# ScalarE copies the next batch's keys behind the exponentials in the first layer

## What is computed

```python
a = _layer_norm(audio_kv, ln_gamma, ln_beta)          # 8 x 1500 x 256
Q = (hidden_states @ Wq.T).reshape(B, Tt, HEADS, HEAD_DIM).transpose(0, 2, 1, 3)
K = (a @ Wk.T).reshape(B, Ta, HEADS, HEAD_DIM).transpose(0, 2, 1, 3)
V = (a @ Wv.T).reshape(B, Ta, HEADS, HEAD_DIM).transpose(0, 2, 1, 3)
scores = jnp.einsum('bhtd,bhsd->bhts', Q, K) * scale
attn = jax.nn.softmax(scores, axis=-1)
out = jnp.einsum('bhts,bhsd->bhtd', attn, V)
return hidden_states + jnp.tanh(gate) * out
```

## Time and profile before

| | |
|---|---|
| Median of 3 runs | 1822.67 us (1819.48 to 1823.98) |
| The profiled execution, timed as the runs are | 1822.74 us |
| Its span, first to last instruction | 1820.9 us |
| PE busy | 1671.2 us (92%), mean granted clock 0.973 |
| DVE busy | 1214.3 us (67%) |
| ACT busy | 1041.7 us (57%) |
| POOL busy | 898.0 us (49%) |
| Mean DMA rate over the span | 82 GB/s |

### The profile page before, as it was taken

How to read it: one execution, slowest core, us unless ns; L and a number is a source line. 1 busy time by engine, 2 the same in 40 slices (tenths; PEclk the granted TensorE clock), 3 DMA queues, 4 the chain that set the end, 5 groups by cost and what they waited for, 6 DMA issues and landing times.

```text
span 1820.9 us, 40621 instructions
## 1 busy us (share of the span) xinstructions
PE 1671.2 (92%) x12520; PEld 1571.5 (86%) x12520; DVE 1214.3 (67%) x2334; ACT 1041.7 (57%) x2023; POOL 898.0 (49%) x655
## 2 busy tenths in 40 slices
PE   3698889887798999999999999989999999999997
PEld 2577777776688999999999997789999999999986
DVE  5477777766546667667766767466676676677673
ACT  2476666656454566565655656545565665656563
POOL 4455555533234365355445547544554653554483
PEclk8899999999889999999999999999999999999998
DMA  7766676775322111001101104221111010010021
GB/s 228 210 146 166 157 178 175 175 171 118 90 64 81 43 34 67 34 34 67 35 33 67 49 23 140 64 78 35 57 58 43 34 67 34 34 67 0 1 88 42
DMA packets 109911, 149.69 MB, mean 82 GB/s; under 512 B 25540, under 2 KB 95684, under 8 KB 109828
## 3 DMA queue, kind: packets, MB, share of 16 engines
q1 hardware_dynamic: 108484, 142.45, 28.0%
q10 hardware_dynamic: 1344, 6.19, 1.0%
HBM read 108.32 MB, written 3.42 MB: 61 GB/s over the span
## 4 chain that ended last, share of the span: by engine, by line
PE 63%; DVE 9%; SPq 6%; issue 4%; ACT 3%; DMA 2%; POOL 2%; DVEq 0%; ACTq 0%; POOLq 0%
PE ps L765 11%; PE ps L767 11%; PE ps L766 11%; PE ps L1016 7%; PE ps L1020 7%; PE ps L1018 7%; SPq L389 4%; PE ps L951 2%; DMA q<-q_scratch 2%; DVE ar L1851 1%; PE ps L996 1%; PE ps L983 1%; SPq L392 1%; DVE negm L1879 1%; ACT prob L1292 1%
## 5 line engine op out<-in xcount | busy, mean ns | idle before, releaser
L717 POOL TENSOR_TENSOR rr<-ar,rr 125x512 fp32r<-125x512 f32 x336 | 450.8, 1376 | 417.1 <-ACT rr L1474 401.1
L1016 PE MATMUL ps<-cx,rr 125*128 125x258 f32 x1344 | 395.5, 294 | 0.0
L1020 PE MATMUL ps<-cx,rr 125*128 125x258 f32 x1344 | 379.3, 282 | 0.0
L1018 PE MATMUL ps<-cx,rr 125*128 125x256 f32 x1344 | 379.2, 282 | 0.0
L765 PE MATMUL ps<-rr,ct 128*125 128x256 f32 x1152 | 330.6, 287 | 4.5 <-DVE ar L1896 2.7
L767 PE MATMUL ps<-rr,ct 128*125 128x256 f32 x1152 | 325.2, 282 | 0.0
L766 PE MATMUL ps<-rr,ct 128*125 128x256 f32 x1152 | 324.9, 282 | 0.0
L1018 PEld LDWEIGHTS ps<-cx,rr 125*128 125x128 f32 x1344 | 254.7, 190 | 0.0
L1020 PEld LDWEIGHTS ps<-cx,rr 125*128 125x128 f32 x1344 | 254.7, 190 | 0.0
L1016 PEld LDWEIGHTS ps<-cx,rr 125*128 125x128 f32 x1344 | 253.6, 189 | 0.1
L1461 ACT ACTIVATE ar<-ar 125x512 f32<-125x512 f32 x336 | 208.6, 626 | 78.2 <-DVE ar L1896 54.5
(11 more groups left out here) (210 smaller groups left out, 3743.2 us busy)
## 6 DMA issues: line engine op xcount, KB each, us to landing
raw_t<-in_ctx_t SPq DMA_DIRECT2D x24, 1500.0 KB, 6.3
k<-khl SPq DMA_DIRECT2D x192, 187.5 KB
raw<-in_ctx SPq DMA_DIRECT2D x16, 1500.0 KB
raw<-in_ctx SPq DMA_DIRECT2D x8, 1408.0 KB
raw<-stat_scratch ACTq DMA_DIRECT2D x7, 750.0 KB, 3.9
w_raw<-in_wq SPq DMA_DIRECT2D x32, 128.0 KB, 2.3
w_raw<-in_wk SPq DMA_DIRECT2D x32, 128.0 KB, 2.2
qo<-in_wqt SPq DMA_DIRECT2D x32, 128.0 KB, 2.4
```

Source lines behind the costliest of these rows:

```text
L717: pool.tensor_tensor(group(p[:, 1, :, :], u, k), x, f(group(p[:, 0, :, :], u, k)), ALU.subtract)\
L1016: pe.matmul(ps[:, bank, 0:D + 2], hi, cx[0:KC, c, 0:D + 2], start=c == 0, stop=False, skip_group_check=True)
L1018: pe.matmul(ps[:, bank, 0:D], hi, cx[0:KC, c, D + 2:CW], start=False, stop=False, skip_group_check=True)
L1020: mm = pe.matmul(ps[:, bank, 0:D + 2], lo, cx[0:KC, c, 0:D + 2], start=False, stop=c == CH - 1, skip_group_check=True)
```

## The change

In ACT's `slot` the copy of the keys moves from ahead of the exponential to behind the exponential and `output`. It issues the same instructions with the same waits. It applies in slots 0 to 5 of batches 0 to 6, 42 copies. The other engines' programs are unchanged.

```diff
--- before.py
+++ after.py
@@ -1335,10 +1335,6 @@
                     if u_last == 0 and later:
                         act.wait_ge(s["zpv"], SLOTS * b)
                     values(b + 1 if t else b, u_last, 1 - n if t else n, 6)
-                if t in K_AT and kind != "plain":
-                    u = K_N[t]
-                    act.wait_ge(s["zkl"], 6 * (b + 1) + u - 4)
-                    keys(b + 1, u, 5)
                 if kind == "full" and t == 4:
                     spread_stats(b + 2)
                 if not (kind == "plain" and t == SLOTS - 1):
@@ -1347,6 +1343,10 @@
                     softmax(n if t < SLOTS - 1 else 1 - n, (t + 1) % SLOTS, g + 1)
                 if t or later:
                     output(g - 1)
+                if t in K_AT and kind != "plain":
+                    u = K_N[t]
+                    act.wait_ge(s["zkl"], 6 * (b + 1) + u - 4)
+                    keys(b + 1, u, 5)
                 high_probs(g, 0)
                 high_probs(g, 1)
                 if kind == "full":
```

## The result

| | before | changed |
|---|---|---|
| Median | 1823.98 us (1818.86 to 1831.35, 7 runs) | 1834.23 us (1827.15 to 1845.85, 7 runs) |
| Ratio to before | | 1.0066 [1.0039, 1.0093] |
| Profiled execution | 1822.74 us | 1827.37 us |
| Its span and mean granted clock | 1820.9 us, 0.973 | 1825.5 us, 0.970 |

The sign of the likeliest case was right, its size was not: +4.85 us forecast, about +10 to +12 us measured by medians and ratio. The profiled execution of the changed kernel is +4.63 us on the profiled one of before, but it is the second fastest of its seven, so that agreement is worth little. The seven changed runs also line up with their clocks: 1827.15 us at 0.969, 1845.85 us at 0.957.

A forecast was written before the change was run, and what follows sets the result against it. It took a 50.3 us loop through SP's stacks, POOL and L775 to bound the first layer. +6.65 at batch 6's landing, −2.1 and +0.3 gave +4.85 us on 1822.74 (median 1822.67), forecast 1827.6, range 1821 to 1832.

The forecast's parts named there:

- the likeliest case: Whole kernel: the sum of terms as it stands, +4.85 us to 1827.6 us, spanning 1825 to 1830.5; chance 45%.
- The loop, its owner and the step of 1.70 us: First layer: SP's stacks, POOL, L775 and the keys' copy form a 50.3 us loop; slot 4's later copy adds 1.70.
- The exponential: ACT: starts 0.6 us earlier in slot 4, 0.35 us in other slots, saving 0.35 at L775 in batches 0 to 2.
- rival B: L775: longer waits drop PE's clock, each fall costing about 2 us; one gives 1829.7, two 1831.8; chance 25%.
- the sum: First layer: +6.65 us at the landing in batch 6, −2.1 given back, +0.3 for pair 0, making +4.85 us.
- the slack of batches 0 to 2: L775 of batches 1 and 2 still waits for DVE, so full 1.70 us steps add only from batch 4 on.
- the give-back in batch 6: Batch 6: PE no longer waits for the exponential behind the copy, returning 1.6 to 2.6 us, taken as 2.1.
- The wait for pair 0: Batch 7's first scores: SP's stack of pair 0 comes 1.7 us later, costing 0 to 1.7 us, taken as 0.3.
- C: Stacks: transfers bound them, not SP's issuing; earlier statistics broadcast shortens the burst by 1.2 us; 1821.9 us; chance 13%.
- D: Stacks: the stretch to the last landing gives up 1.7 us, landings don't move, only gains remain; 1819.8 us; chance 10%.
- The range: Whole kernel: 1821 to 1832 us, leaving out D and the far end of rival B.

The follow-up runs named there:

- e1: Changed kernel with the keys' copy back ahead of the exponential in slot 4 only; 1824.94 us, 1.0010 of the kernel before.
- e2: Kernel before with the keys' copy behind the exponential in slot 4 alone; 1837.51 us, 1.0078 of the kernel before.
- e8: Kernel before with one extra, unused subtraction on POOL ahead of slot 4's key block; 1827.01 us, 1.0023 of the kernel before.
- e6: Changed kernel with eight unused matmuls on PE ahead of L775 in batches 0 to 5; 1832.59 us, 1.0045 of the kernel before.
- e13: Changed kernel with eight unused matmuls on PE ahead of L775 in batches 1 to 5 only; 1833.56 us, 1.0048 of the kernel before.
- e15: Second measurement of the changed kernel with eight unused matmuls ahead of L775 in batches 0 to 5; 1833.45 us, 1.0043 of the kernel before.
- e3: The changed kernel measured and profiled once more, nothing else altered; 1839.85 us, 1.0071 of the kernel before.
- e5: Kernel before with POOL's variance of slot 2 computed ahead of its third key block and `ra`; 1819.58 us, 0.9975 of the kernel before.
- e11: Kernel before with POOL's variance early and six unused matmuls in PE's waits of slot 6; 1818.93 us, 0.9965 of the kernel before.
- e12: Second measurement of the kernel before with POOL's variance ahead of its third key block and `ra`; 1818.51 us, 0.9967 of the kernel before.
- e4: Changed kernel with POOL's variance of slot 2 computed ahead of its third key block and `ra`; 1822.78 us, 1.0000 of the kernel before.
- e14: Changed kernel with eight unused matmuls ahead of L775 in batches 1 to 5 and six in slot 6; 1838.62 us, 1.0064 of the kernel before.

## Why the prediction was wrong

**The loop, its owner and the step of 1.70 us: right.** Landing to SP's start went from 14.53 to 16.27 us, POOL's wait in slot 4 from 3.19 to 4.88 us (forecast 4.9), and e1 and e2 put the loss on slot 4. e8 made a third of it without ACT. Starts 52.0 us apart were forecast from batch 2 on and are there on average where the clock holds behind L775 (52.0 to 52.1 us in e6, e13, e15).

**The exponential: its shift right, and worth nothing.** It came 0.6 us earlier in slot 4. L775 waited 0.57 us for DVE in batch 1 in place of 0.88, as forecast, but that wait had no weight once POOL was the last. e1, which keeps the earlier exponential in the other slots, gains nothing (1.0010).

**Step that failed, the largest: the clock behind L775 (rival B at 25%, with one or two falls, and left out of the sum).** I let a single row decide, the wait of 3.00 us at 401.38 that left the clock at full, and gave B a quarter. The runs show a fall behind the loop's longer waits at L775 as a rule: two in the first profile of the changed kernel, five in e3, four in e2. The price of one, "about 2 us", was right: 1.3 to 2.3 us from landing to SP's start. Their number was not. Holding the clock there gives back some 3 to 5 us. The Trainium skill, TensorE: Matmul & The Clock Gate, Part 1: The HAM clock gate, has the clock go back to 1.2 GHz when the array idles; I quoted it as making B near certain, and here the rows of 2.90, 3.57, 3.79 and 4.19 us agree with it. No wait of that length at L775 did as the row at 401.38 had done.

**Step that failed, second: the slack of batches 0 to 2.** I let the loop take hold in batch 3, since batch 0 showed 34.36 us from SP's start to the landing and batch 1 34.67. Over the 17 profiles of this case the stretch of batch 0 is 34.03 to 37.11 us and 35.61 on average, that of batch 1 34.67 to 37.16 and 36.02: one of my two was among the shortest, the other the shortest of all. With the average of batch 0, L775 of batch 1 waits for POOL already, which takes 1.15 us out of the slack; with that of batch 1, L775 of batch 2 does too, another 0.95 us. The last landing then moves by 8.75 us, not 6.65 (an estimate, from the averages and the prediction's own rules). So it is in e3 (152.82, 2.99 us for POOL) and in e15, where batch 0 to batch 1 takes 52.24 us, in place of the 50.7 (50.14 + 0.55) that I had worked out. In e6, e15 and e13 the last landing lies 7.5, 7.8 and 7.9 us behind before's profile.

**Step that failed, third: the give-back in batch 6, taken as 2.1 us.** The exponential no longer makes PE wait, as forecast, but the end doesn't come earlier. From the last landing to the layer's end it is 74.2 us in the first profile of the changed kernel in place of 75.3. That one profile misleads: over the eleven profiles that have the copy behind the exponential in slots 3 and 5 it is 74.1 to 77.1 us and 75.6 on average, over the five with the old order (before, e5, e8, e11, e12) 74.8 to 75.8 and 75.4. I had forecast 1.8 us less. All eleven have a wait for the low part of the probabilities in its place, 1.68 to 4.86 us at L847 (3.00 in e3, 3.34 in e15), and none of the five has one. The wait for pair 0 stands in four of the eleven (0.30 to 1.71 us), which fits the 0.3 on average.

**The sum again.** 4.85, plus 2.1 for the slack and 1.8 for a give-back that isn't there, is 8.75 us. The kernels with the clock held at L775 stand at +7.8 to +8.8 us by their ratios, and end the layer 6.2, 6.7 and 9.3 us behind before's profile (490.6, 491.0, 493.7). The falls at L775 add 3 to 5, and 12 to 14 is where the changed kernel measured +12 and +13 us by its two ratios. So nothing large is left over, but each of these terms is known to 1 us at best.

**C and D** are out: no stretch of stacks gave up anything (34.03, 37.07, 35.53, 34.53 and 36.04 us against 34.36, 34.67, 36.58, 35.78 and 36.01), and the broadcast of the statistics issued earlier didn't shorten it. Single stretches of 32.9 to 33.9 us do occur (e1, e6, e8, e4, e11, one batch each), with the copy in either place.

**The range** reached from C to two falls of B. With a fall in each of batches 1 to 5, at the prediction's own 2.1 us, its end would have been 1838 us and would have held the time; nothing in the profile limited their number to two. And the sum was set against one profile whose clock (0.973) and first two stretches were all on the good side.

## What to carry to other kernels

Follow an instruction that you move through what is queued behind it on the other engines as well, and see whether that closes a loop: here the moves in five slots of six were free, and the one in front of POOL's split and SP's in-order queue cost 1.7 us every batch. When a loop lengthens, the bounding engine's waits lengthen with it, so count what its clock does behind each of them, not behind one or two. And before a term rests on slack read from one batch of one profile, read the same stretch in all batches: here the slack hung on 34.36 and 34.67 us, and the other three of the five were 1.1 us or more longer. The same holds for a gain: a wait that goes away is one only if no other stands behind it.

## What the runs showed of the hardware that I had not expected

- Idle time can be filled at a profit: eight extra matmuls (1.96 us of TensorE) inside a wait held the granted clock at 1.00 where it had fallen to 0.50, and the kernel took about 4 us less (32 runs against 18). It doesn't always hold: in e14 the clock fell behind two such waits of 2.05 and 1.98 us all the same.
- What a fall costs depends on who is last. Where TensorE's own way bounds the loop, one in slot 6 made it 1.3 to 1.8 us longer (e5: SP's starts 51.8 us apart against 49.8 to 50.4). Where POOL comes last, it only made the wait at L775 shorter (1.30 us in the changed kernel behind the stretches of 220 to 228 us).
- Waits of nearly the same length aren't followed by the same clock: 1.70 and 1.71 us at L775 with a fall (e3, e2), 1.84 and 1.87 us without (e2, the changed kernel); 3.00 us at full (401.38 in the kernel before), 2.90 us with 0.68 on average over the stretch (205.21 in the changed one).
- With 18 extra matmuls a batch in PE's loop, its second pass began with 6.42 us in which TensorE waited for nothing that the profile shows; with 14 it did not. The cause wasn't measured.
